# The tail of a two-layer adaptive FFN kernel behind its last convolution: six edits to the order of work

## The chip, the cores and the metric

One core of one Trainium2 chip runs the whole program. The metric is the device time of one execution in microseconds (us); the median of three runs is quoted.

## The reference, cut to what matters

The input x is 128 samples of 32 channels by 512 values. Layer 0 adds to x a gated low-rank product. Layer 1 is what this change touches:

```python
o = conv1d(x1, weight, groups=4, 9 taps) + ctx[:, :, None] + bias      # x1: x after layer 0
xf = o.reshape(-1, 512); N = 4096; capacity = int(3.0 * N / 8)         # 1536
h = relu(layernorm(xf @ gw1.T + gb1) * gamma + beta)
gates = h @ gw2.T + gb2
top_v, top_i = top_k(gates, 2); top_g = softmax(top_v)
onehot = (top_i[..., None] == arange(8)); counts = onehot.sum(axis=0)  # over all 4096 rows
w = einsum('nke,nk,ke->ne', onehot, top_g, counts <= capacity)
out = x1 + xf @ weight.T + einsum(lora_A product * w, lora_B) / 16
```

`counts` runs over every row of the input. So no row's LoRA term can be finished before the routing of the last row is known. The kernel therefore has a loop over all rows and then a separate LoRA stage.

## The kernel before, in words

**Tiling.** A tile is 128 rows (4 samples by 32 channels) by 512 columns, 256 KB. Four tiles (t = 0 to 3) are a step, and there are eight steps (s = 0 to 7). All of y = x1 + main product stays in the on-chip tensor `y_all`, the lora_A products in `tmp_all`, the routing weights in `wst_all`. Each engine has its own instruction list, ordered by hand; semaphores are the only ties between them.

**The loop.** `steps` runs a step function over s. In step 7 and in a closing pass `s == NS` (8) the engines do only what is left: TensorE (PE) finishes convolutions, the gate products `gates(t)`, the transposes of the normed hidden values (`hidden_transposed`), the router product, and the main products. `main(7, t)` is twelve matmuls of 512 columns; their results lie in the banks `ps_last[t]`. `main(7, 2)` is in `ps_t`, `main(7, 1)` and `main(7, 3)` in two `ps_d` banks. A high-and-low split into two fp32r parts (hi is a rounded copy, lo is what is left) gives fp32 quality with three matmuls.

**VectorE (DVE) in step 7.** `norm_first(7)` makes the variance; GpSimd (POOL) takes its root (`rstd`, L483); `y_out(7, 0)` adds a main product into y; `choices_counted(6)` makes the one-hot tensor `oh` (L897) and adds its sums to `cnt` (L904, L905); `norm_last(7)` (L938) scales the hidden values, for which PE waits (L1336); then `choices_weighted(6)`. In the closing pass it makes the choices of step 7.

**ScalarE (ACT) and POOL in step 7.** The last thing that ACT does there is `lb_hi`, a rounded copy of lora_B (L728); POOL's last is the remainder `lb_lo` (L536). `lb_hi` lies in `b_hi`, `lb_lo` in `o1l[0]`.

**Counts.** Behind `main(7, 2)` PE multiplies a matrix of ones with `cnt` (L1464) and four times with a tile of `oh` (L1467), all summed in one bank. In plain fp32 each product is two passes in the trace. `main(7, 3)` follows.

**Behind the loop, DVE:** `allowed` (L1030), the weights of step 0 (L1036, L1037, L1041 which PE transposes), those of step 1 (L1036, L1037, then POOL's product L543), `choices_weighted(7)` (L911 to L915), the weights of steps 2 to 7 (L1036, L1037), then `y_out(7, 1)`, `y_out(7, 2)`, `y_out(7, 3)` (L862) and `lt_lo[0]` (L1051), the remainder of the first transposed weights.

**The LoRA stage.** For each of eight steps PE transposes the weighted products of the next step (L1480) and does three matmuls a tile: `high` (L1487 with `lb_hi`, L1488 with `lb_lo`) and `low` (L1491). In step 0 it does high(0), high(1), low(0), low(1), then waits until all of y is ready and goes on with tiles 2 and 3. ACT makes the transposed hi (L767), POOL the lo (L555). DVE's `finish` adds y to each tile (L1062) and SyncE (SP) stores it (L424).

Of the kernel before, what the change touches and what calls it, by code (L numbers as in the profile page):

```python
# [12 lines left out]
def adaln_ffn_kernel(nc: bass.Bass, x, cond, fside, w0, b0, w1, b1, w2, b2, mixw, mixb, ffa, ffb, ffr,  # L13
# [7 lines left out]
    P = 128  # L21
# [31 lines left out]
    with ctx:  # L53
# [48 lines left out]
        v = sb("v", [P, NT, UC])  # L102
        gms = sb("gms", [P, NT, 2, ER0])
        gm = sb("gm", [P, NT, ER0])
# [74 lines left out]
        def pb(name):  # L179
# [80 lines left out]
        lb_hi, lb_lo = b_hi, o1l[0][:, :, :].rearrange("p q m -> p (q m)")  # L260
        yo = [[xT[:, t, :, :].rearrange("p c m -> p (c m)") for t in range(NT)],
# [64 lines left out]
        def _(sp):  # L326
# [94 lines left out]
            def store(s, par, k):  # L421
                for t in range(NT):
                    sp.wait_ge(s_yo[t], s + 1)
                    sp.dma_start(out_v[bass.ds(s * NT + t, 1)].rearrange("n p h -> p (n h)"), yo[par][t])\  # L424
                      .then_inc(s_out[par][t], 16)
            steps(sp, store, 0, NS - 1)
            for par in range(2):
                for t in range(NT):
                    sp.wait_ge(s_out[par][t], 16 * (NS // 2))

        @block.gpsimd
        def _(pool):
# [77 lines left out]
            def step(s, par, k):  # L510
                if at_step(s, -1):
                    for t in (1, 3):
                        pool.wait_ge(s_x1, t + 1)
                        pool.tensor_copy(xq0[t], y_all[:, t * H:(t + 1) * H].rearrange("p (m q) -> p q m", q=Q))\
                            .then_inc(s_x1q0[t], 1)
                    mixing(1)
                    pool.wait_ge(s_gah, 1)
                    pool.wait_ge(s_gm, 2)
                    pool.tensor_tensor(wt_lo[:, :, H:H + GC], ga[:, :, :], wt_hi[:, :, H:H + GC].bitcast(fp32),
                                       ALU.subtract).then_inc(s_gal, 1)  # L520
                    o1_low(0, 0)
                    return
                if has(s, 2):
                    mixing(s + 2)
                o1_low(s, 1)
                if has(s, -1):
                    rstd(s - 1)
                o1_low(s, 2)
                o1_low(s, 3)
                if has(s, 1):  # L530
                    o1_low(s + 1, 0)
                if at_step(s, NS - 1):
                    rstd(s)
                    pool.wait_ge(s_lbh, 1)
                    pool.wait_ge(s_mp, s * NT + 1)
                    pool.tensor_tensor(lb_lo, lbn, lb_hi[:, :].bitcast(fp32), ALU.subtract).then_inc(s_lb, 1)  # L536
# [23 lines left out]
        def _(act):  # L560
# [81 lines left out]
            def step(s, par, k):  # L642
# [72 lines left out]
                if at_step(s, NS - 1):  # L715
# [58 lines left out]
        def _(dve):  # L774
# [3 lines left out]
            def gates0(u):  # L778
# [27 lines left out]
                wait(dve, s_gtp, u)  # L806
                link(V.tensor_copy(gms[:, :, 0, :].bitcast(fp32r), gm[:, :, :]))
                V.tensor_tensor(gms[:, :, 1, :], gm[:, :, :], gms[:, :, 0, :], ALU.subtract).then_inc(s_gm, 1)
                assert n[0] == N_C0, n[0]
# [83 lines left out]

            def choices_counted(u):
                link, n = chain(dve, s_c2, u * N_C2 + N_C2A)
# [51 lines left out]
            def step(s, par, k):  # L947
# [43 lines left out]
                if at_step(s, NS - 1):  # L991
# [26 lines left out]
                if has(s, -1):  # L1018
# [27 lines left out]
            allow(2, NS).then_inc(s_w, 1)  # L1046
            y_out(NS - 1, 1)
            y_out(NS - 1, 2)
            y_out(NS - 1, 3)
            dve.wait_ge(s_lth, 1)  # L1050
            V.tensor_tensor(lt_lo[0][:, :], ps_a[0][:, :], lt_hi[0][:, :].bitcast(fp32), ALU.subtract)\  # L1051
             .then_inc(s_ltf, 1)


            dve.wait_ge(s_y, NS * NT)

            def finish(s, par, k):
                if has(s, 0):
                    for t in range(NT):
                        dve.wait_ge(s_lp, s * NT + t + 1)  # L1060
                        wait(dve, s_out[par][t], k * 16)
                        V.tensor_tensor(yo[par][t], ps_l[t][:, :], y_all[:, bass.ds(s * ST + t * H, H)],  # L1062
                                        ALU.add).then_inc(s_yo[t], 1)
            steps(dve, finish, 0, NS - 1)

        @block.tensor
        def _(pe):
# [216 lines left out]
            def step(s, par, k):  # L1284
# [31 lines left out]
                def gm_transposed(u):  # L1316
# [6 lines left out]
                    for t in range(NT):  # L1323
                        last = T.transpose(ps_t[:, t * P:(t + 1) * P],
                                           gms[:, t, :, :].rearrange("p a c -> p (a c)"), idp)
                    last.then_inc(s_gtp, 1)
# [147 lines left out]
            def lora(s, par, k):  # L1474
# [8 lines left out]

                def high(t):
                    wait(pe, s_yo[t], s)
                    lhs = lt_hi[par][:, t * P:(t + 1) * P]
                    T.matmul(ps_l[t][:, :], lhs, lb_hi[:, :], start=True, stop=False)  # L1487
                    T.matmul(ps_l[t][:, :], lhs, lb_lo, start=False, stop=False)  # L1488

                def low(t):  # L1490
                    T.matmul(ps_l[t][:, :], lt_lo[par][:, t * P:(t + 1) * P], lb_hi[:, :],  # L1491
                             start=False, stop=True).then_inc(s_lp, 1)
# [17 lines left out]
                if has(s, 0):  # L1510
                    pe.wait_ge(s_ltl, s)
                    for t in range(NT):
                        high(t)
                        low(t)
            steps(pe, lora, -1, NS - 1)

# [25 lines left out]
```

## Time and profile before

| | us |
|---|---|
| median of 3 runs | 305.33 |
| lowest and highest | 303.22, 305.46 |
| the profiled execution | 303.87 |
| its span, first to last instruction | 302.1 |
| PE busy in the span | 290.3 (96%) |
| DVE busy | 194.9 (64%) |
| mean granted TensorE clock | 0.997 |

The busy time of PE counts pipelined matmuls whole, so 96% is how seldom PE stood still, and not how near it was to its peak. 1.73 us of the profiled execution lie around the span.

### The profile page before, as it was taken

How to read it: one execution, taken by the hardware profiler on the slowest of the kernel's cores; microseconds unless marked ns; L12 is line 12 of the kernel's file. 1: busy time of each engine (PE TensorE's matmuls, PEld its weight loads, DVE VectorE, ACT ScalarE, POOL GpSimd, SP SyncE). 2: the span in 40 equal slices, each digit the busy share in tenths (PEclk: the TensorE clock that was granted, in tenths of full speed). 3: DMA queues.
4: the chain of work that ended last, by engine and by line, in shares of the span. 5: the costliest groups of instructions: out<-in, count | busy, mean ns of one | idle time of the engine just before them, and what ended most of it. 6: DMA issues, size and time to landing. Idle time of an engine off the chain costs nothing.

```text
span 302.1 us, 6171 instructions
## 1 busy us (share of the span) xinstructions
PE 290.3 (96%) x1995; PEld 239.7 (79%) x1995; DVE 194.9 (64%) x503; ACT 125.2 (41%) x263; POOL 95.1 (31%) x124
## 2 busy tenths in 40 slices
PE   7999999999999999999999999999999999798994
PEld 6989967787888788879887978797868777586883
DVE  1445984734488448835793579366957645878785
ACT  3417743436523652356235622562256235111330
POOL 4342425132312331143114311431114116216650
PEclk9999999999999999999999999999999999999998
DMA  5696799992779289918892879386538860004887
GB/s 134 196 335 139 169 257 220 235 217 62 218 214 208 54 220 229 192 35 243 207 201 44 242 205 189 55 233 148 136 71 244 174 142 0 0 2 171 322 334 286
DMA packets 74255, 52.75 MB, mean 175 GB/s; under 512 B 44388, under 2 KB 61204, under 8 KB 74232
## 3 DMA queue, kind: packets, MB, share of 16 engines
q1 hardware_dynamic: 72792, 51.37, 67.3%
q10 hardware_dynamic: 1120, 1.07, 1.2%
q0 software_dynamic: 320, 0.02, 0.4%
q8 instruction: 12, 0.20, 0.3%
q14 instruction: 11, 0.09, 0.1%
HBM read 35.67 MB, written 16.78 MB: 174 GB/s over the span
## 4 chain that ended last, share of the span: by engine, by line
PE 65%; SPq 10%; DVE 10%; DMA 6%; issue 4%; ACT 2%; DVEq 0%; ACTq 0%
PE ps_g L1124 13%; PE ps_d L1124 12%; PE ps_c L1264 8%; PE ps_a L1085 6%; PE ps_t L1280 4%; SPq L352 4%; DMA xg<-x1d 3%; PE ps_a L1074 3%; DMA x1d<-xq 3%; PE ps_d L1305 3%; SPq L355 2%; PE ps_d L1306 2%; PE ps_v L1097 2%; PE ps_d L1491 1%; PE ps_d L1487 1%
## 5 line engine op out<-in xcount | busy, mean ns | idle before, releaser
L508 POOL TENSOR_TENSOR o1l<-o,o1h 128x512 fp32r<-128x512 f32 x30 | 39.3, 1311 | 149.3 <-ACT o L639 149.3
L1124 PE MATMUL ps_d<-wt_hi,o1h 128*128 128x336 f32 (+1 forms) x120 | 41.1, 342 | 0.3 <-DVE y_all L950 0.3
L1124 PE MATMUL ps_d<-wt_hi,o1l 128*128 128x336 f32 (+1 forms) x120 | 38.7, 323 | 0.0
L1124 PE MATMUL ps_d<-wt_lo,o1h 128*128 128x336 f32 (+1 forms) x120 | 38.6, 322 | 0.0
L1124 PE MATMUL ps_g<-wt_hi,o1h 128*128 128x336 f32 x112 | 35.7, 319 | 0.6 <-ACT tmp_all L654 0.4
L944 DVE TENSOR_TENSOR oT<-ps_c,biasT 128x512 f32<-128x512 f32 x32 | 21.9, 685 | 21.7 <-PE ps_c L1264 21.7
L1124 PE MATMUL ps_g<-wt_hi,o1l 128*128 128x336 f32 x112 | 35.5, 317 | 0.0
L1124 PE MATMUL ps_g<-wt_lo,o1h 128*128 128x336 f32 x112 | 35.4, 316 | 0.0
L1264 PE MATMUL ps_c<-xg,cw 96*32 96x512 f32 x256 | 34.1, 604 | 1.0 <-DMA xg<-x1d 1.0
L627 ACT ACTIVATE xq<-y_all 128x512 f32 (+1 forms) x29 | 31.8, 1150 | 7.0 <-DMA x1d<-xq 3.7
L1085 PEld LDWEIGHTS ps_a<-pm,xT 128*128 128x128 f32 x256 | 30.2, 192 | 1.4 <-issue 0.8
L1085 PE MATMUL ps_a<-pm,xT 128*128 128x68 f32 x256 | 30.6, 273 | 0.1
L950 DVE TENSOR_TENSOR y_all<-ps_d,xs 128x512 f32 (+1 forms) x24 | 15.9, 689 | 17.9 <-PE ps_d L1306 17.9
L653 ACT ACTIVATE hs<-ps_g 128x32 f32<-128x32 f32 x32 | 6.2, 195 | 49.9 <-DVE y_all L870 49.6
L1280 PEld LDWEIGHTS ps_t<-ident,oT 128*128 128x128 f32 x128 | 14.5, 144 | 15.3 <-issue 14.3
L1124 PEld LDWEIGHTS ps_d<-wt_hi,o1h 128*128 128x128 f32 x120 | 22.7, 189 | 1.0 <-issue 0.7
L1124 PEld LDWEIGHTS ps_d<-wt_lo,o1h 128*128 128x128 f32 x120 | 22.6, 189 | 0.2
L1124 PEld LDWEIGHTS ps_d<-wt_hi,o1l 128*128 128x128 f32 x120 | 22.5, 188 | 0.3
L637 ACT ACTIVATE o1h<-ps_t 128x512 fp32r<-128x512 f32 x30 | 18.0, 599 | 11.1 <-PE ps_t L1280 11.1
L1124 PEld LDWEIGHTS ps_g<-wt_hi,o1h 128*128 128x128 f32 x112 | 21.1, 188 | 1.8 <-issue 1.8
L574 ACT ACTIVATE xT<-ps_a 128x512 f32<-128x512 f32 x32 | 18.2, 604 | 8.1 <-PE ps_a L1074 8.0
L1124 PEld LDWEIGHTS ps_g<-wt_lo,o1h 128*128 128x128 f32 x112 | 21.0, 188 | 0.0
(249 smaller groups left out, 582.1 us busy)
## 6 DMA issues: line engine op xcount, KB each, us to landing
xg<-x1d SPq DMA_DIRECT2D x64, 254.0 KB, 4.8
xg<-x1d SPq DMA_DIRECT2D x32, 256.0 KB, 3.7
x1d<-xq SPq DMA_DIRECT2D x30, 256.0 KB, 3.4
xs<-in_x_dram SPq DMA_DIRECT2D x6, 1024.0 KB, 5.9
out_dram<-xT SPq DMA_DIRECT2D x16, 256.0 KB, 2.1
out_dram<-xg SPq DMA_DIRECT2D x16, 256.0 KB, 2.1
y_all<-in_x_dram ACTq DMA_DIRECT2D x2, 512.0 KB, 5.5
y_all<-in_x_dram SPq DMA_DIRECT2D x1, 1024.0 KB, 5.7
```

The costliest lines, as they stand in the source:

```text
L352: sp.dma_start(taps[i:C:Q, :, 7 - i:7 - i + TAPS], convw.rearrange("o c k -> c o k")).then_inc(s_ld["conv"], 16)
L508: pool.tensor_tensor(lo, o1[t % 2][:, :, :], hi.bitcast(fp32), ALU.subtract).then_inc(s_o1l, 1)
L574: nc.scalar.activation(xT[:, t, :, :].rearrange("p c m -> p (c m)"), ps_a[t % 2][:, :], ACT.Copy).then_inc(s_xt, 1)
L627: nc.scalar.activation(dst, y_all[:, bass.ds(u * ST + t * H, H)].rearrange("p (m q) -> p q m", q=Q), ACT.Copy).then_inc(done, 1)
L637: nc.scalar.activation(o1h[t % 2][:, :, :].rearrange("p q (b o) -> p q b o", o=CG), o_in(t), ACT.Copy).then_inc(s_o1h, 1)
L944: V.tensor_tensor(oT[:, t % 2, :, :], ps_c[:, :].rearrange("p (b m) -> p b m", b=BT), row(biasT[:, bass.ds(u * (NT * BT) + t * BT, BT)], 2 ...
L950: V.tensor_tensor(y_all[:, bass.ds(u * ST + t * H, H)], ps_d[t % 2][:, :], src[:, t, :], ALU.add).then_inc(s_x1, 1)
L1074: last = T.transpose(ps_a[t % 2][:, c * P:(c + 1) * P], bank_x[:, t, c * P:(c + 1) * P], idp)
L1085: last = T.matmul(ps_a[0][:, t * UC:(t + 1) * UC], xT[:, t, c, :], pm[:, c, :], start=(c == 0), stop=(c == HC - 1))
L1124: last = T.matmul(bank[:, 0:columns], a[:, Q - 1 - q, :], w[:, q, first:first + columns], start=(q == 0 and n == 0), stop=(q == Q - 1 and ...
L1264: last = T.matmul(ps_c[C * g:C * g + C, :], cw[0:KC, g, :, :].rearrange("p q o -> p (q o)"), xg[0:KC, t % 2, :, g, :], start=True, stop=True)
L1280: last = T.transpose(ps_t[:, b * P:(b + 1) * P], oT[:, t % 2, b, :], idp)
```

## The change

1. In step 7 `norm_last(7)` runs inside `choices_counted(6)`, ahead of the two instructions that sum `oh` into `cnt`.
2. The four count products on `oh` become one of 64 columns, and `cnt` has columns of its own. DVE now sums the five groups of 16 columns (one new instruction) before the comparison.
3. `y_out(7, 1)` and `y_out(7, 2)` go ahead of the allowed chain on DVE, and `y_out(7, 3)` goes behind `lt_lo[0]`.
4. `lb_hi` and `lb_lo` are made in step 6: ACT's copy ahead of the last `ga_out` of that step, POOL's remainder at the end of its step. `lb_lo` moves to the tensor `gms`, which is declared fp32r for it.
5. The last tile of the LoRA stage is made in two halves of 256 columns, the second in bank `ps_t`: six matmuls in place of three, two additions and two stores in place of one each.

```diff
@@ GpSimd, end of a step
                 if at_step(s, NS - 1):
                     rstd(s)
+                if at_step(s, NS - 2):
                     pool.wait_ge(s_lbh, 1)
-                    pool.wait_ge(s_mp, s * NT + 1)
+                    pool.wait_ge(s_gtp, NS)
                     pool.tensor_tensor(lb_lo, lbn, lb_hi[:, :].bitcast(fp32), ALU.subtract).then_inc(s_lb, 1)
@@ ScalarE, step 7 and the steps before it
                     ga_out(3)
-                    act.wait_ge(s_ld["lora"], 16)
-                    nc.scalar.activation(lb_hi[:, :], lbn, ACT.Copy).then_inc(s_lbh, 1)
                     return
...
                 o_hi(s + 1, 0)
+                if at_step(s, NS - 2):
+                    act.wait_ge(s_ld["lora"], 16)
+                    nc.scalar.activation(lb_hi[:, :], lbn, ACT.Copy).then_inc(s_lbh, 1)
                 ga_out(3)
@@ VectorE
                     link(chosen)
+                    if between is not None:
+                        between()
                     link(V.reduce_sum(cnt1[:, :, :], oh[:, :, :, :].rearrange("p t c e -> p c e t"), AXX))
...
-                    choices_counted(s - 1)
-                    norm_last(s)
+                    choices_counted(s - 1, lambda: norm_last(s))
                     choices_weighted(s - 1)
...
+            y_out(NS - 1, 1)
+            y_out(NS - 1, 2)
             link, n = chain(dve, s_c3, 0)
             dve.wait_ge(s_cntp, 1)
-            link(V.tensor_scalar(allowed[:, :, :], ps_g[:, 0:2 * E1].rearrange("p (c e) -> p c e", c=2),
-                                 float(CAPACITY), None, ALU.is_le))
+            link(V.reduce_sum(cnt1[:, :, :], ps_g[:, 0:2 * E1 * (NT + 1)]
+                              .rearrange("p (t c e) -> p c e t", c=2, e=E1), AXX))
+            link(V.tensor_scalar(allowed[:, :, :], cnt1[:, :, :], float(CAPACITY), None, ALU.is_le))
...
             allow(2, NS).then_inc(s_w, 1)
-            y_out(NS - 1, 1)
-            y_out(NS - 1, 2)
-            y_out(NS - 1, 3)
             dve.wait_ge(s_lth, 1)
             V.tensor_tensor(lt_lo[0][:, :], ps_a[0][:, :], lt_hi[0][:, :].bitcast(fp32), ALU.subtract)\
              .then_inc(s_ltf, 1)
+            y_out(NS - 1, 3)
...
+                        parts = 2 if at_step(s, NS - 1) and t == NT - 1 else 1
+                        n = H // parts
+                        for i in range(parts):
+                            dve.wait_ge(s_lp, s * NT + t + i + 1)
+                            V.tensor_tensor(yo[par][t][:, i * n:i * n + n], (ps_l[t], ps_t)[i][:, i * n:i * n + n],
+                                            y_all[:, bass.ds(s * ST + t * H + i * n, n)],
+                                            ALU.add).then_inc(s_yo[t], 1)
@@ TensorE
-            T.matmul(ps_g[:, 0:2 * E1], ones[:, :], cnt[:, :, :].rearrange("p c e -> p (c e)"), start=True, stop=False)
+            T.matmul(ps_g[:, 2 * E1 * NT:2 * E1 * (NT + 1)], ones[:, :], cnt[:, :, :].rearrange("p c e -> p (c e)"),
+                     start=True, stop=True)
             pe.wait_ge(s_cnt, 1)
-            for t in range(NT):
-                last = T.matmul(ps_g[:, 0:2 * E1], ones[:, :], oh[:, t, :, :].rearrange("p c e -> p (c e)"),
-                                start=False, stop=(t == NT - 1))
-            last.then_inc(s_cntp, 1)
+            T.matmul(ps_g[:, 0:2 * E1 * NT], ones[:, :], oh[:, :, :, :].rearrange("p t c e -> p (t c e)"),
+                     start=True, stop=True).then_inc(s_cntp, 1)
...
+                if at_step(s, NS - 1):
+                    for cols, bank in ((slice(0, H // 2), ps_l[NT - 1]), (slice(H // 2, H), ps_t)):
+                        high(NT - 1, cols, bank)
+                        low(NT - 1, cols, bank)
```

Left out of the diff here: `store` on SP issues the last tile's two halves as two DMAs, and the casts that the new type of `gms` asks for.

## Rows read from the trace of the kernel before

**Rows 1.** Stretches: length, busy PE, PEld, DVE, ACT, POOL, granted clock, DMA share, GB/s

```profile
272.40:273.90 1.50, 0.19 (x2) 0.01 (x1) 1.44 (x3) 0.00 (x0) 1.50 (x3) 1.00 0.00 0
...
274.50:298.30 23.80, 23.73 (x115) 18.93 (x113) 21.01 (x32) 6.52 (x12) 12.18 (x11) 1.00 0.85 317
...
300.00:300.50 0.50, 0.00 (x0) 0.00 (x0) 0.00 (x0) 0.00 (x0) 0.00 (x0) 0.78 1.01 393
```

**Rows 2.** Timeline of step 7: start, length, engine, line, shape [idle before <-releaser]

```profile
256.78 0.63 ACT L728 ACTIVATE b_hi<-xs 128x512 fp32r<-128x512 f32 x1
...
259.00 1.01 POOL L483 TENSOR_TENSOR small<-small,mhalf 128x4 f32<-128x4 f32 x1 [3.76 <-DVE small L931]
...
259.98 1.26 POOL L536 TENSOR_TENSOR o1l<-xs,b_hi 128x512 fp32r<-128x512 f32 x1
...
260.20 1.07 DVE L905 TENSOR_TENSOR cnt<-cnt 128x16 f32<-128x16 f32 x1
...
261.19 0.28 DVE L938 TENSOR_TENSOR hr<-hb,small 128x128 f32<-128x128 f32 x1
...
261.53 0.33 PE L1336 MATMUL ps_a<-ident,hr 128*128 128x128 f32 x1 [1.55 <-DVE hr L938]
...
262.92 0.19 DVE L882 TENSOR_TENSOR sc<-ps_v,gb_b 128x32 f32<-128x32 f32 x1 [0.58 <-PE ps_v L1342]
```

**Rows 3.** All instructions of a line: nanoseconds min/median/max, starts, forms

```profile
L905 DVE TENSOR_TENSOR cnt<-cnt x7: 174/176/1069, 94.7 to 260.2; 128x16 f32<-128x16 f32 x7
...
L904 DVE TENSOR_REDUCE cnt<-oh x7: 257/258/261, 94.4 to 259.9; 128x16 f32<-128x64 f32 x7
```

**Rows 4.** Timeline of PE from the counts to the first transposes

```profile
265.97 0.39 PE L1124 MATMUL ps_t<-wt_hi,wt_lo 128*128 128x512 f32 x1
...
266.31 0.97 PEld L1467 LDWEIGHTS ps_g<-oh,ones 128*128 128x128 f32 x8
...
267.20 0.19 PEld L1124 LDWEIGHTS ps_d<-wt_hi,gmT 128*128 128x128 f32 x1
...
269.87 1.03 PEld L1480 LDWEIGHTS ps_a<-ident,xs 128*128 128x128 f32 x8
```

**Rows 5.** Timeline of DVE and POOL behind the counts

```profile
267.49 0.17 DVE L1030 TENSOR_SCALAR allowed<-ps_g 128x16 f32<-128x16 f32 x1 [1.84 <-PE ps_g L1467]
...
268.19 0.69 DVE L1041 TENSOR_TENSOR xs<-tmp_all,wst_all 128x512 f32<-128x512 f32 x1
...
269.32 1.06 POOL L543 TENSOR_TENSOR xs<-tmp_all,wst_all 128x512 f32<-128x512 f32 x1 [8.08 <-DVE wst_all L1037]
...
271.08 0.36 DVE L1037 TENSOR_TENSOR wst_all<-wst_all 128x192 f32<-128x192 f32 x1
...
271.36 0.68 DVE L862 TENSOR_TENSOR y_all<-ps_d,y_all 128x512 f32<-128x512 f32 x1
...
273.16 0.68 DVE L1051 TENSOR_TENSOR wt_lo<-ps_a,wt_hi 128x512 fp32r<-128x512 f32 x1
```

**Rows 6.** Timeline of PE, first tiles of the LoRA stage

```profile
271.39 0.50 PE L1487 MATMUL ps_c<-b_hi,wt_hi 128*128 128x512 f32 x1 [0.25 <-ACT wt_hi L767]
...
271.72 0.39 PE L1488 MATMUL ps_c<-o1l,wt_hi 128*128 128x512 f32 x1
...
273.89 0.50 PE L1491 MATMUL ps_c<-b_hi,wt_lo 128*128 128x512 f32 x1 [1.31 <-DVE wt_lo L1051]
...
274.69 0.40 PE L1488 MATMUL ps_d<-o1l,wt_hi 128*128 128x512 f32 x1
```

**Rows 7.** Timeline of step 6's end: ACT and POOL

```profile
247.16 0.20 ACT L653 ACTIVATE hs<-ps_g 128x32 f32<-128x32 f32 x1 [2.98 <-DVE y_all L870]
...
249.53 1.28 POOL L508 TENSOR_TENSOR o1l<-o,o1h 128x512 fp32r<-128x512 f32 x1 [3.98 <-ACT o L639]
```

**Rows 8.** The load of lora_B by its source line

```profile
L408 SPq DMA_DIRECT2D xs<-in_L_ffn_lora_B_dram x1: 340/340/340, 205.1 to 205.1; - x1
```

**Rows 9.** Timeline of DVE: an addition of 336 columns out of PSUM

```profile
244.95 0.51 DVE L867 TENSOR_TENSOR y_all<-ps_d,y_all 128x336 f32<-128x336 f32 x1 [1.72 <-PE ps_d L1124]
```

More of the change, by code:

```diff
@@ L102, in adaln_ffn_kernel @@
         v = sb("v", [P, NT, UC])
-        gms = sb("gms", [P, NT, 2, ER0])
+        gms = sb("gms", [P, NT, 2, ER0], fp32r)
         gm = sb("gm", [P, NT, ER0])
@@ L259, in adaln_ffn_kernel @@
                                       for i in range(2)]
-        lb_hi, lb_lo = b_hi, o1l[0][:, :, :].rearrange("p q m -> p (q m)")
+        lb_hi, lb_lo = b_hi, gms[:, :, :, :].rearrange("p t a c -> p (t a c)")
         yo = [[xT[:, t, :, :].rearrange("p c m -> p (c m)") for t in range(NT)],
@@ L422, in store @@
                 for t in range(NT):
-                    sp.wait_ge(s_yo[t], s + 1)
-                    sp.dma_start(out_v[bass.ds(s * NT + t, 1)].rearrange("n p h -> p (n h)"), yo[par][t])\
-                      .then_inc(s_out[par][t], 16)
+                    parts = 2 if at_step(s, NS - 1) and t == NT - 1 else 1
+                    n = H // parts
+                    for i in range(parts):
+                        sp.wait_ge(s_yo[t], s + i + 1)
+                        sp.dma_start(out_v[bass.ds(s * NT + t, 1)].rearrange("n p h -> p (n h)")[:, i * n:i * n + n],
+                                     yo[par][t][:, i * n:i * n + n]).then_inc(s_out[par][t], 16)
             steps(sp, store, 0, NS - 1)
@@ L428, in _ @@
                 for t in range(NT):
-                    sp.wait_ge(s_out[par][t], 16 * (NS // 2))
+                    sp.wait_ge(s_out[par][t], 16 * (NS // 2 + (par == 1 and t == NT - 1)))
         @block.gpsimd
@@ L806, in gates0 @@
                 wait(dve, s_gtp, u)
-                link(V.tensor_copy(gms[:, :, 0, :].bitcast(fp32r), gm[:, :, :]))
-                V.tensor_tensor(gms[:, :, 1, :], gm[:, :, :], gms[:, :, 0, :], ALU.subtract).then_inc(s_gm, 1)
+                link(V.tensor_copy(gms[:, :, 0, :], gm[:, :, :]))
+                V.tensor_tensor(gms[:, :, 1, :], gm[:, :, :], gms[:, :, 0, :].bitcast(fp32),
+                                ALU.subtract).then_inc(s_gm, 1)
                 assert n[0] == N_C0, n[0]
@@ L892, in choices_first, with choices_counted @@
                 assert n[0] == N_C2A, n[0]
-            def choices_counted(u):
+            def choices_counted(u, between=None):
                 link, n = chain(dve, s_c2, u * N_C2 + N_C2A)
@@ L1059, in finish @@
                     for t in range(NT):
-                        dve.wait_ge(s_lp, s * NT + t + 1)
                         wait(dve, s_out[par][t], k * 16)
-                        V.tensor_tensor(yo[par][t], ps_l[t][:, :], y_all[:, bass.ds(s * ST + t * H, H)],
-                                        ALU.add).then_inc(s_yo[t], 1)
+                        parts = 2 if at_step(s, NS - 1) and t == NT - 1 else 1
+                        n = H // parts
+                        for i in range(parts):
+                            dve.wait_ge(s_lp, s * NT + t + i + 1)
+                            V.tensor_tensor(yo[par][t][:, i * n:i * n + n], (ps_l[t], ps_t)[i][:, i * n:i * n + n],
+                                            y_all[:, bass.ds(s * ST + t * H + i * n, n)],
+                                            ALU.add).then_inc(s_yo[t], 1)
             steps(dve, finish, 0, NS - 1)
@@ L1324, in gm_transposed @@
                         last = T.transpose(ps_t[:, t * P:(t + 1) * P],
-                                           gms[:, t, :, :].rearrange("p a c -> p (a c)"), idp)
+                                           gms[:, t, :, :].bitcast(fp32).rearrange("p a c -> p (a c)"), idp)
                     last.then_inc(s_gtp, 1)
@@ L1482, in weighted_transposed, with high, low @@
                     last.then_inc(s_ltp, 1)
-                def high(t):
+                def high(t, cols=slice(0, H), bank=None):
                     wait(pe, s_yo[t], s)
                     lhs = lt_hi[par][:, t * P:(t + 1) * P]
[L1487 to L1491, printed above, removed]
+                    bank = bank or ps_l[t]
+                    T.matmul(bank[:, cols], lhs, lb_hi[:, cols], start=True, stop=False)
+                    T.matmul(bank[:, cols], lhs, lb_lo[:, cols], start=False, stop=False)
+                def low(t, cols=slice(0, H), bank=None):
+                    bank = bank or ps_l[t]
+                    T.matmul(bank[:, cols], lt_lo[par][:, t * P:(t + 1) * P], lb_hi[:, cols],
                              start=False, stop=True).then_inc(s_lp, 1)
@@ L1511, in lora @@
                     pe.wait_ge(s_ltl, s)
-                    for t in range(NT):
+                    for t in range(NT - 1 if at_step(s, NS - 1) else NT):
                         high(t)
                         low(t)
+                if at_step(s, NS - 1):
+                    for cols, bank in ((slice(0, H // 2), ps_l[NT - 1]), (slice(H // 2, H), ps_t)):
+                        high(NT - 1, cols, bank)
+                        low(NT - 1, cols, bank)
             steps(pe, lora, -1, NS - 1)
```

## The prediction, made before the changed kernel was run

> **What bounds the kernel now.** I read the granted clock first: it is full until the last matmul, so the clock explains nothing. Then the timeline of the tail, where brackets give an engine's idle time and who ended it, and the busy time by stretch. From step 7 on TensorE (PE) is the bound, with two real holes. The first is 1.55 us ahead of the transposes of the normed values (L1336), released by DVE's L938 [rows 2]. The second is 1.31 us ahead of low(0) (L1491), released by DVE's `lt_lo` L1051 [rows 6]; in that stretch PE is busy 0.19 of 1.50 us [rows 1]. A third cost is no hole but small work: ten weight loads for the counts between `main(7, 2)` and `main(7, 3)`. Behind 274.5 PE is busy 23.73 of 23.80 us [rows 1]: the LoRA stage takes its PE time, whenever it begins. So the change is worth what it lets PE begin that stage earlier, plus or minus the last store.
>
> Why the first hole is as long as it is can be read from four rows. POOL's root ends at 260.01, and `norm_last` needs only that. But ahead of it on DVE stands L905, 16 elements, which takes 1.07 us from 260.20, while the line's median is 0.176 us [rows 2, 3]. POOL's `lb_lo` (L536) runs from 259.98 to 261.24, and L905 ends when it ends [rows 2]. L904, which starts in the same stretch, has its usual length in all seven executions [rows 3]. The Trainium skill, page "SBUF — State Buffer", section "Who interferes with whom", says that a DVE instruction with two SBUF inputs and a GpSimd one that reads SBUF block each other for a whole instruction, and that a reduction never does. The trace agrees for both lines.
>
> **Edits 1 and 4, norm ahead of the counts and the split earlier.** Each alone would remove most of the hole: with L536 gone L905 is short, and with L938 ahead of it its length doesn't delay PE. Together L938 starts as soon as the root is there: 260.01 + 0.03 = 260.04 in place of 261.19, 1.15 us earlier, and the transposes start at 260.38. PE has nothing to do from 259.98, so the gain is on its path: **1.15 us**. About 0.4 us of the hole stay. Behind L938 now stand L904 and L905, 0.26 and 0.18 long [rows 3], ahead of the weights of step 6. With L938 at 260.04 the weights begin at about 260.75. Before they began right behind L938, at 261.4. So they gain some 0.65 us where PE gains 1.15, and the other 0.5 comes out of the 0.58 us that DVE was idle ahead of the last choices [rows 2]. That idle time just suffices.
>
> The moved work: ACT's copy of 0.63 us and POOL's of 1.26 us [rows 2]. In step 6 ACT is idle for 2.98 us up to 247.16 and POOL for 3.98 us up to 249.53 [rows 7]. The copy fits at 244.2 to 244.8. POOL's previous instruction ends at 249.53 - 3.98 = 245.55, so `lb_lo` fits until 246.8, 2.7 us ahead of POOL's next work. The load of lora_B was issued at 205.1 [rows 8], some 39 us ahead, so ACT's new wait holds up nothing: behind it stand `ga_out(3)` and the next `o_hi`, and PE waits for those. DVE's additions there read one tensor in PSUM. Cost: **0**; without this cover up to 0.63 + 1.26 = 1.89 us. The semaphore waits that allow the new places (step 7's gate transposes done) are passed on PE early in step 6, so they cost nothing.
>
> **Edit 2, counts.** Ten passes become four. Eight weight loads take 267.20 - 266.31 = 0.89 us [rows 4], 0.11 each, so six fewer give **0.67 us** on PE. The pass of 64 columns isn't in the trace: at least 0.11 (16 columns), at most the 23.80 / 115 = 0.21 us of a mostly 512-column stretch [rows 1]; two passes then cost up to 0.2 more. I take 0.11, since 64 is nearer to 16. PE's first transposes behind `main(7, 3)` move from 269.87 [rows 4] by 1.15 + 0.67 = 1.82 us to 268.05.
>
> DVE pays for it with a reduction of 80 elements out of PSUM. The nearest rows are the reduction L904 of 64 elements, 0.26 us [rows 3], below it a comparison of 16 out of PSUM, 0.17, and above it an addition of 192 elements, 0.36 [rows 5]. L904 is nearest: I take 0.28, and 0.03 to the next instruction, **0.31 us**, with 0.17 and 0.4 as bounds.
>
> **Edit 3, the additions.** Before, DVE is idle for 1.84 us until 267.49 for the counts [rows 5]. `y_out(7, 1)` fits in there whole. `y_out(7, 2)` needs `main(7, 2)`, whose last matmul ends at 265.97 + 0.39 = 266.36 [rows 4], less 1.15 = 265.21, and starts at 265.26. Three additions take 273.16 - 271.36 = 1.80 us [rows 5], so 0.60 each, and the reduction starts at 265.86. The counts are in PSUM at about 265.6, so this addition costs the chain some 0.2 to 0.3 us. Then `allowed` starts at 265.86 + 0.31 = 266.17, **1.32 us** earlier than 267.49. L1041 ends at 268.88 - 1.32 = 267.56 and PE wants it at 268.05, so it still doesn't wait. POOL's L543 moves with the chain, from 269.32 to 268.00, and ends at 269.06; PE's second transposes wait for it and end at 269.6, when high(0) begins (before: 271.39 [rows 6]).
>
> From here on DVE is late, and it decides. Its last L1037 starts at 271.08 - 1.32 = 269.76, and what follows it at 271.36 - 1.32 = 270.04 [rows 5]. Before, that was three additions and then L1051 at 273.16. Now it is L1051 itself: 270.04, **3.12 us** earlier. PE's low(0) goes from 273.89 to 270.77, while its high products are done at 270.4: 0.4 us of the hole of 1.31 stay. `y_out(7, 3)` starts 0.60 later, at 270.64, and ends at 271.32. PE waits for all of y ahead of high(2) and is done with low(1) at 271.1, so a new wait of 0.2 to 0.3 us opens. High(2) starts at 271.39; a first matmul behind a wait delays the next by 0.33 (271.39 to 271.72 [rows 6]), so its second is at 271.73 in place of 274.69 [rows 6]: **2.96 us**. The sum on PE is 1.82, and the rest, 1.14, comes from the second hole, of which small pieces of wait remain.
>
> **Edit 5, halves.** PE and DVE: an addition of 512 columns takes 0.68 and one of 336 columns 0.51 [rows 5, 9], so 256 take about 0.43. DVE's second half ends about when the whole tile did, 298.97 in the old time. The second store has half the bytes, worth up to 0.35 us. But the DMA engines are fully busy from 300.0 to 300.5, at 393 GB/s [rows 1], more than a microsecond after DVE is done: the last step's stores wait for bandwidth and not for DVE. At that rate 256 KB take 0.67 us, as long as DVE takes to make them. The bytes are the same, so I take **0**, bounds -0.35 and +0.2 (double the packets, at half the size). The Trainium skill, page "SBUF — State Buffer", section "Summary: rules for kernel authors", gives about 358 GB/s for transfers to HBM. By that figure a tile would take, as an estimate, 0.73 us, and halves would give nothing either; the trace shows somewhat more than the page.
>
> **The sum.** 2.96 + 0 = 2.96 us off the profiled 303.87, which is 300.91. The profiled execution lies 1.46 under the median; the saving is taken off the median: 305.33 - 2.96 = **302.4**.
>
> **The rivals.**
> (a) DVE's chain is longer than I have it. It decides from `main(7, 2)` on, with no slack, so each 0.1 us there is 0.1 at the end: a reduction of 0.4, and L905 slow for a reason of its own. Then `oh` of step 7 comes 0.9 - 0.1 = 0.8 later and with it the first addition, at 265.3 in place of 264.5, so the reduction starts at 266.6 in place of 265.86. For it: L905 alone carries the proof of POOL's hold. Against it: its median in six other steps [rows 3]. L905 slow would give 2.96 - 0.75 = 2.2 us saved, 303.1; both of it 2.1, 303.2.
> (b) The stores gain. The halves shorten the last landing by 0.35, and a DMA engine that ran behind the others doesn't: 3.3 to 3.6 saved, 301.7 to 302.0. Against it: the full DMA share [rows 1].
> (c) The change doesn't do its work in the LoRA stage: if the stores bounded it, an earlier begin would give nothing but the wait to the end. Against it: a DMA share of 0.85 beside 23.73 of 23.80 on PE [rows 1]. 0 saved, 305.3.
> (d) Slower than before: the moved split is in the way in step 6. POOL takes its list in order, so `lb_lo` waiting for ACT holds back `o1_low(7, 1)`, `main(7, ...)` and all behind. It decides if `lb_hi` comes later than 244.8 + 2.7 = 247.5, and loses more than is gained from 250.5 on, which a late load of lora_B or ACT stuck behind its wait could do; at 252 it costs 4.5 - 2.96 = 1.5 us, 306.9. Against it: 39 us between issue and use [rows 8], and the idle times [rows 7].
>
> **How the numbers follow.** Forecast 0.64, (a) 0.17, (b) 0.12, (c) 0.03, (d) 0.04. For the range: (b) at the low end and (a) at the high end, and the median of before lies anywhere between 303.22 and 305.46, which moves the end results by a microsecond downward: 300.3 to 304.3. One per cent is 3.05 us, about what a measurement of this kernel can tell from no change, and the forecast of 2.96 lies just under it. Of its 0.64 the scatter of some 0.3 us puts 0.28 above and 0.36 below; with (b) above, and (a), (c) and the milder part of (d) within: faster by over 1% 0.40, within 1% 0.57, slower 0.03.
>
> **What would show it.** L938 starts within 0.1 us of the end of POOL's root, L905 takes 0.18 us, PE idles about 0.4 us ahead of L1336. Four weight loads stand between the main products of tiles 2 and 3. `allowed` is preceded by one reduction of about 0.3 us and no idle time of DVE. low(0) is 3.1 us earlier and high(2) has a short wait for DVE's y. The last store's landing moves with PE's last matmul. I am wrong if any DVE instruction behind the counts is stretched, if ACT or POOL wait in step 6, or if the last landing doesn't follow PE.

## The result, and the profile after

The changed kernel takes 301.05 us (median of 7, 300.46 to 302.11), the kernel before 305.01 us (median of 7, 303.22 to 308.09). The ratio is 0.9895 with a 95% interval of 0.9863 to 0.9927: 1.05% faster. The profiled execution took 301.39 us with a span of 299.7; before it was 303.87 and 302.1. Disturbed executions, more than 1.5% above the fastest of the same kernel, are left out of all ratios, among them the 308.09 us of the kernel before; without it the median of that kernel is 304.28 us.

Absolute times of two executions differ by some tenths before the change begins, so I count from the start of POOL's root of step 7: 259.00 before [rows 2], 259.22 after. **D** is the time from there to the second matmul of high(2): 274.69 - 259.00 = 15.69 us before [rows 6].

The timeline of the changed kernel, around the last norm; L946 is the old L938, L913 the old L905, L1348 the old L1336:

```profile
259.22 1.01 POOL L486 TENSOR_TENSOR small<-small,mhalf 128x4 f32<-128x4 f32 x1 [3.75 <-DVE small L939]
...
260.32 0.29 DVE L946 TENSOR_TENSOR hr<-hb,small 128x128 f32<-128x128 f32 x1 [0.22 <-POOL small L486]
...
260.66 0.33 PE L1348 MATMUL ps_a<-ident,hr 128*128 128x128 f32 x1 [0.47 <-DVE hr L946]
...
260.81 0.17 DVE L913 TENSOR_TENSOR cnt<-cnt 128x16 f32<-128x16 f32 x1
```

DVE's L946 starts 1.10 us behind the root's start, where L938 started 2.19 behind it [rows 2]. L913 takes 0.17 us and not 1.07. PE idles 0.47 us and not 1.55.

The same timeline behind the counts. L1039 is the new reduction, L1041 `allowed`, L547 POOL's weights of step 1, L923 the last step of `choices_weighted(7)`, L1058 `lt_lo`, L868 `y_out`, L1504, L1499 and L1500 low, high with `lb_hi` and high with `lb_lo`:

```profile
265.55 0.69 DVE L868 TENSOR_TENSOR y_all<-ps_t,y_all 128x512 f32<-128x512 f32 x1
...
266.16 0.23 DVE L1039 TENSOR_REDUCE cnt<-ps_g 128x16 f32<-128x80 f32 x1
...
266.43 0.17 DVE L1041 TENSOR_SCALAR allowed<-cnt 128x16 f32<-128x16 f32 x1
...
268.26 1.06 POOL L547 TENSOR_TENSOR xs<-tmp_all,wst_all 128x512 f32<-128x512 f32 x1 [8.03 <-DVE wst_all L1047]
...
268.82 0.58 DVE L923 SCALAR_TENSOR_TENSOR wst_all<-exs,small 128x64 f32<-128x64 f32 x1
...
269.37 0.66 PE L1491 MATMUL ps_a<-ident,xs 128*128 128x128 f32 x4 [0.19 <-POOL xs L547]
...
270.30 0.68 DVE L1058 TENSOR_TENSOR wt_lo<-ps_a,wt_hi 128x512 fp32r<-128x512 f32 x1
...
270.90 0.68 DVE L868 TENSOR_TENSOR y_all<-ps_d,y_all 128x512 f32<-128x512 f32 x1
...
271.04 0.50 PE L1504 MATMUL ps_c<-b_hi,wt_lo 128*128 128x512 f32 x1
...
271.64 0.50 PE L1499 MATMUL ps_d<-b_hi,wt_hi 128*128 128x512 f32 x1
...
271.98 0.40 PE L1500 MATMUL ps_d<-gms,wt_hi 128*128 128x512 f32 x1
```

Nothing on DVE waits between 265.55 and 270.90: it is the bound there. One piece of it is the hold of step 7 once more. L923 has 64 elements and two SBUF inputs; it takes 0.58 us beside POOL's L547, which ends at 269.32, and 0.23 us as the median of its eight executions. The kernel before has the same 0.58. So some 0.35 us of DVE's deciding chain may still be had; no run tried it. `lt_lo` starts 11.08 us behind the root in place of 14.16 [rows 5]. D is 271.98 - 259.22 = 12.76 us, **2.93 us less** than before; the forecast was 2.96.

The busy time by stretch (columns as in [rows 1]):

```profile
271.64:295.60 23.96, 23.86 (x118) 19.38 (x117) 21.17 (x32) 6.52 (x12) 14.01 (x12) 1.00 0.85 315
...
297.50:298.00 0.50, 0.00 (x0) 0.00 (x0) 0.00 (x0) 0.00 (x0) 0.00 (x0) 1.00 0.93 309
...
298.00:298.50 0.50, 0.00 (x0) 0.00 (x0) 0.00 (x0) 0.00 (x0) 0.00 (x0) 1.00 0.07 12
```

The LoRA stage is as before, PE busy 23.86 of 23.96 us, DMA share 0.85. Its last PE instruction ends 36.28 us behind the root (before 39.24), again 2.96 less. The span ends 2.70 us earlier (40.44 behind the root, before 43.14), so 0.26 us are lost behind PE, and the row from 298.0 on shows a thin tail of transfers (the last two figures of a row are the DMA share and GB/s).

### The profile page after: what moved, and what is told of

Same layout as the page of the kernel before. It is cut to its first block, busy times and chain, and to the rows that moved or that the text cites. A ratio compares the mean times of both kernels' runs of the same rounds, so it can differ in the third digit from the quotient of the medians.

```text
span 299.7 us, 6154 instructions
## 1 busy us (share of the span) xinstructions
PE 289.8 (97%) x1992; PEld 239.0 (80%) x1992; DVE 194.4 (65%) x505; ACT 125.3 (42%) x263; POOL 95.2 (32%) x124
## 3 DMA queue, kind: packets, MB, share of 16 engines
q10 hardware_dynamic: 1120, 1.07, 1.2%
## 4 chain that ended last, share of the span: by engine, by line
PE 66%; SPq 10%; DVE 8%; DMA 6%; issue 4%; ACT 2%; POOL 1%; DVEq 0%; ACTq 0%
PE ps_g L1136 13%; PE ps_d L1136 12%; PE ps_c L1276 8%; PE ps_a L1097 7%; PE ps_t L1292 4%; DMA xg<-x1d 3%; SPq L352 3%; PE ps_a L1086 3%; DMA x1d<-xq 3%; PE ps_d L1317 3%; SPq L355 2%; PE ps_d L1318 2%; PE ps_v L1109 2%; PE ps_d L1499 1%; PE ps_d L1504 1%
```

## The experiments

Each was run beside the kernel before on the same chip. D and the other distances are counted from the start of the root of step 7 in its own trace.

### The split of lora_B alone

```diff
@@ kernel before: edit 4 only
-                    pool.wait_ge(s_mp, s * NT + 1)
+                if at_step(s, NS - 2):
+                    pool.wait_ge(s_gtp, NS)
```

> The kernel before with edit 4 alone (lora_B split in step 6). Measure D: from the start of POOL's root of step 7 to the second matmul of high(2) in the LoRA stage; before 274.69 - 259.00 = 15.69 us. Theory (POOL's subtraction holds back L905): L905 takes 0.18 us, L938 starts 0.8 us earlier, D = 14.9, time 0.8 us under before. Rival (L905 is slow there for a reason of its own): L905 still takes about 1 us, D = 15.7, time as before. Rival (the moved split is in the way in step 6): ACT or POOL end their step-6 work later and the root comes later.

Measured: ratio 0.994 [0.9914, 0.9967], which is 1.8 us where 0.8 was expected; most of the excess goes with the clock (under "The median against the profile"), for among the executions with a mean clock above 0.995 the medians are 302.88 and 303.66 us, 0.8 apart. Timeline, L908 being the old L905 and L941 the old L938:

```profile
258.34 1.01 POOL L483 TENSOR_TENSOR small<-small,mhalf 128x4 f32<-128x4 f32 x1 [3.76 <-DVE small L934]
...
259.54 0.18 DVE L908 TENSOR_TENSOR cnt<-cnt 128x16 f32<-128x16 f32 x1
...
259.63 0.28 DVE L941 TENSOR_TENSOR hr<-hb,small 128x128 f32<-128x128 f32 x1
...
259.98 0.33 PE L1339 MATMUL ps_a<-ident,hr 128*128 128x128 f32 x1 [0.66 <-DVE hr L941]
```

L908 takes 0.18 us, so the length of L905 was POOL's doing. L941 starts 1.29 us behind the root (before 2.19), and the transposes 1.64 behind it (before 2.53): 0.89 us earlier. D is 15.28, but in this trace PE ran at half clock for 3.4 us within the stretch (shown below for another run), so D is of no use here. The root comes no later than before (258.34, before 259.00): ACT and POOL had room in step 6.

### The norm ahead of the counts alone

```diff
@@ kernel before: edit 1 only
-                    choices_counted(s - 1)
-                    norm_last(s)
+                    choices_counted(s - 1, lambda: norm_last(s))
```

> The kernel before with edit 1 alone (L938 ahead of L904 and L905; POOL's lb_lo still in step 7). Theory: L938 starts 0.03 us behind the root, PE's transposes 1.15 us earlier; L905 starts near 260.5 and is stretched to POOL's end, so it takes about 0.75 us and not 1.07; the last choices are late by some 0.4 us against PE, and PE has just enough other work; D = 14.6, time 1.1 us under before. Rival (L905 slow for a reason of its own): L905 takes its 1.07 us whole, the one-hot tensor is another 0.3 late and PE waits at the counts, D = 14.9.

Measured: 0.9992 [0.9951, 1.0033], D = 15.63. Neither expectation holds. Timeline, L940 being the old L938:

```profile
259.17 1.01 POOL L483 TENSOR_TENSOR small<-small,mhalf 128x4 f32<-128x4 f32 x1 [3.76 <-DVE small L933]
...
260.15 1.26 POOL L536 TENSOR_TENSOR o1l<-xs,b_hi 128x512 fp32r<-128x512 f32 x1
...
260.27 1.29 DVE L940 TENSOR_TENSOR hr<-hb,small 128x128 f32<-128x128 f32 x1 [0.23 <-POOL small L483]
...
261.61 0.33 PE L1337 MATMUL ps_a<-ident,hr 128*128 128x128 f32 x1 [1.47 <-DVE hr L940]
```

POOL starts its subtraction (L536) at 260.15, DVE its norm at 260.27. L940, which reads two tensors in SBUF, takes 1.29 us in place of 0.28 and ends 0.15 us behind POOL. The blocked instruction is not L905 as such; it is whichever DVE instruction of that kind comes next behind POOL's start. The edit moves the block from L905 to the norm itself, and PE gains 0.09 us.

### The counts alone

```diff
@@ kernel before: edit 2 only
-            for t in range(NT):
-                last = T.matmul(ps_g[:, 0:2 * E1], ones[:, :], oh[:, t, ...])
+            T.matmul(ps_g[:, 0:2 * E1 * NT], ones[:, :], oh[:, :, :, :].rearrange("p t c e -> p (t c e)"), ...)
```

> The kernel before with edit 2 alone (one count product, a reduction on DVE). Theory (behind the counts DVE decides): PE saves 0.67 us, the comparison L1030 starts only 0.3 us earlier since the reduction stands ahead of it, D = 15.4, time 0.3 us under before. Rival (PE's work decides): D = 15.0.

Measured: 0.9986 [0.9956, 1.0016], which agrees with 0.3 us and can't exclude 0.7. D is 16.91, longer than before, and the busy time by stretch of this kernel says why (the granted clock is the third figure from the end):

```profile
259.90:261.40 1.50, 0.00 (x0) 0.00 (x0) 1.47 (x4) 0.00 (x0) 1.26 (x2) 1.00 0.00 0
...
261.50:262.80 1.30, 1.30 (x7) 0.97 (x8) 0.65 (x4) 0.46 (x1) 0.00 (x0) 1.00 0.00 0
...
262.80:266.20 3.40, 3.40 (x9) 2.63 (x9) 2.53 (x9) 0.23 (x1) 0.00 (x0) 0.50 0.00 0
...
266.20:268.00 1.80, 1.80 (x11) 1.50 (x10) 0.00 (x0) 0.00 (x0) 0.00 (x0) 0.99 0.04 9
```

1.4 us behind the first hole the granted clock fell to 0.50, that is 1.2 GHz, for 3.4 us. In that time matmuls of 512 columns start 0.43 us apart, and 0.23 us apart ahead of it and behind it. D can't be read here. The next experiment answers this edit better.

### The changed kernel without the counts' edit

```diff
@@ changed kernel: edit 2 undone
-            link(V.reduce_sum(cnt1[:, :, :], ps_g[:, 0:2 * E1 * (NT + 1)] ...
```

> The changed kernel with edit 2 undone (ten passes for the counts on PE, no reduction on DVE). Theory: PE loses 0.67 us at the counts; DVE waits for them with both additions done, and the comparison starts 0.2 us later than in the changed kernel, 7.4 us behind the root in place of 7.21; D = 13.0 in place of 12.76, so the edit is worth 0.2 to 0.3 us of its 0.67. Rival: D = 13.4.

Measured: 0.992 [0.9881, 0.9959]; D = 13.05, as the theory has it (rival 13.4). The comparison and high(0) start here, the root being at 258.35:

```profile
265.69 0.17 DVE L1039 TENSOR_SCALAR allowed<-ps_g 128x16 f32<-128x16 f32 x1 [0.33 <-PE ps_g L1478]
...
269.66 0.50 PE L1499 MATMUL ps_c<-b_hi,wt_hi 128*128 128x512 f32 x1 [0.25 <-ACT wt_hi L772]
```

The comparison is 7.34 us behind the root, against 7.21 in the changed kernel. High(0) is 11.31 behind it, against 10.65: there the 0.67 us that PE saves are whole. But in the changed kernel the weight loads of low(0) and high(2) then wait 0.41 and 0.30 us for DVE, and in this run for nothing. So the edit is worth 0.3 us of the 0.67, since with it DVE decides, its reduction being part of that chain.

### The additions alone

```diff
@@ kernel before: edit 3 only
+            y_out(NS - 1, 1)
+            y_out(NS - 1, 2)
             link, n = chain(dve, s_c3, 0)
...
             .then_inc(s_ltf, 1)
+            y_out(NS - 1, 3)
```

> The kernel before with edit 3 alone (two additions of y ahead of the comparison, the third behind lt_lo). Theory: both additions fit into DVE's idle 1.84 us, the comparison keeps its place, low(0) follows high(1) without a hole, a short wait of about 0.1 to 0.3 us opens ahead of high(2); D = 14.1, time 1.6 us under before. Rival (the additions delay the comparison by their length): D = 14.7 or more.

Measured: 0.9949 [0.9919, 0.9978]: 1.6 us. In this trace the granted clock was 0.50 from 40.4 to 50.6 us, which is why all of it is later, and 1.00 in the stretch read here. Timeline: the root, the comparison, `lt_lo`, the addition, low(0) and the second matmul of high(2):

```profile
264.69 1.01 POOL L483 TENSOR_TENSOR small<-small,mhalf 128x4 f32<-128x4 f32 x1 [3.77 <-DVE small L931]
...
273.13 0.17 DVE L1032 TENSOR_SCALAR allowed<-ps_g 128x16 f32<-128x16 f32 x1 [0.33 <-PE ps_g L1467]
...
277.09 0.69 DVE L1050 TENSOR_TENSOR wt_lo<-ps_a,wt_hi 128x512 fp32r<-128x512 f32 x1
...
277.70 0.68 DVE L862 TENSOR_TENSOR y_all<-ps_d,y_all 128x512 f32<-128x512 f32 x1
...
278.14 0.40 PE L1491 MATMUL ps_c<-b_hi,wt_lo 128*128 128x512 f32 x1
...
278.85 0.39 PE L1488 MATMUL ps_d<-o1l,wt_hi 128*128 128x512 f32 x1
```

The comparison starts 8.44 us behind the root (8.49 before): both additions fit into DVE's idle time. low(0) has no wait. D = 14.16, 1.53 less than before.

### The changed kernel without the additions' edit

```diff
@@ changed kernel: edit 3 undone
-            y_out(NS - 1, 1)
-            y_out(NS - 1, 2)
             link, n = chain(dve, s_c3, 0)
```

> The changed kernel with edit 3 undone. Theory: DVE's chain decides the end. The comparison starts 0.2 to 0.3 us earlier than in the changed kernel, for y_out(7, 2) no longer stands ahead of the reduction, but three additions stand ahead of lt_lo again; D = 14.2 (changed kernel 271.98 - 259.22 = 12.76), time 1.4 us over the changed kernel. Rival (the PE work saved is worth its 1.82 us by itself): D = 13.9 or less.

Measured: 0.9963 [0.9934, 0.9991], D = 14.27, as expected; the changed kernel's 0.9895 is 2.1 us lower, where 1.4 were expected (among executions with a mean clock above 0.995 the medians are 302.97 and, in the later run of the changed kernel, 301.34, 1.6 apart). The granted clock was 0.50 from 40.2 to 50.5 us and 1.00 in the stretch read here. Timeline: the root, the comparison, `lt_lo` and low(0):

```profile
264.11 1.01 POOL L486 TENSOR_TENSOR small<-small,mhalf 128x4 f32<-128x4 f32 x1 [3.75 <-DVE small L939]
...
271.16 0.17 DVE L1039 TENSOR_SCALAR allowed<-cnt 128x16 f32<-128x16 f32 x1
...
276.83 0.68 DVE L1059 TENSOR_TENSOR wt_lo<-ps_a,wt_hi 128x512 fp32r<-128x512 f32 x1
...
277.57 0.50 PE L1504 MATMUL ps_c<-b_hi,wt_lo 128*128 128x512 f32 x1 [1.62 <-DVE wt_lo L1059]
```

The comparison starts 7.05 us behind the root (7.21 in the changed kernel), `lt_lo` 12.72 (11.08), and the hole ahead of low(0) is 1.62 us, longer than before any change. PE alone had saved 1.8 us; 1.42 of D come out.

### The last tile whole, twice

```diff
@@ changed kernel: edit 5 undone
-                    parts = 2 if at_step(s, NS - 1) and t == NT - 1 else 1
+                    parts = 1
```

> The changed kernel with edit 5 undone (last tile whole). Theory (the last step's stores wait for DMA bandwidth): the last landing keeps its distance to PE within 0.1 us, and the time is that of the changed kernel within 0.2 us. Rival (halves shorten the end): 0.35 us longer. Rival (halves cost, by double the packets and a second issue): 0.2 us shorter.

Measured: 300.2 us, ratio 0.9861 [0.9833, 0.9888], where the changed kernel has 0.9895. To settle it both were run again side by side:

> The changed kernel as it is, beside its variants on one chip. It and whole_again answer whether the halves cost something: whole_last_tile measured 0.9861 [0.9833, 0.9888] of before, the changed kernel 0.9895 [0.9863, 0.9927]. Theory (bandwidth): the two agree within 0.2 us, and what differed was one DMA engine that ended 0.67 us behind the others in one profile and not in the other. Rival (halves cost): this kernel is 0.5 to 0.9 us slower than whole_again.

> The changed kernel with edit 5 undone, once more, beside after_again. Theory: its time within 0.2 us. Rival (halves cost): 0.5 to 0.9 us under after_again, and all 16 DMA engines end together again where the changed kernel has one that ends 0.67 us behind.

Measured: halves 301.34 us, 0.9895 [0.9856, 0.9933]; whole 300.37 us, 0.9862 [0.9826, 0.9899]. In 13 executions with halves the fastest took 300.41 us, in 12 with the tile whole the slowest took 300.93, and the medians differ by 0.85 and 0.97. The theory of no effect falls: the kernel with halves is 0.9 us slower. PE is not it: D is 12.74 and 12.75, and PE's last instruction ends 36.32 and 36.31 us behind the root. The busy time by stretch shows the difference, first with halves (root at 259.21):

```profile
297.60:297.90 0.30, 0.00 (x0) 0.00 (x0) 0.00 (x0) 0.00 (x0) 0.00 (x0) 1.00 1.04 348
...
298.20:298.50 0.30, 0.00 (x0) 0.00 (x0) 0.00 (x0) 0.00 (x0) 0.00 (x0) 0.63 0.09 14
...
298.50:298.80 0.30, 0.00 (x0) 0.00 (x0) 0.00 (x0) 0.00 (x0) 0.00 (x0) 0.50 0.04 10
```

then with the tile whole (root at 258.95):

```profile
297.60:297.90 0.30, 0.00 (x0) 0.00 (x0) 0.00 (x0) 0.00 (x0) 0.00 (x0) 1.00 0.17 55
...
297.90:298.20 0.30, 0.00 (x0) 0.00 (x0) 0.00 (x0) 0.00 (x0) 0.00 (x0) 0.71 0.00 0
```

With halves the transfers thin out instead of ending: a share of 0.04 to 0.09 is about one of 16 engines at work, until 298.73. Fifteen engines have ended 38.89 us behind the root, the last one ends at 39.53. With the tile whole the sixteen end between 38.66 and 38.82, the last one 0.03 us behind the fifteenth. So of the 0.71 us between the last landings 0.64 are one DMA engine that is behind, and 0.1 is the rest. The trace doesn't name the engine of a packet, but it names the queue. The changed kernel from 290 to 299:

```profile
q1 hardware_dynamic: 1707, 2.84, 86.0%
...
q14 instruction: 1, 0.01, 0.3%
```

and with the tile whole until its last landing:

```profile
q1 hardware_dynamic: 1526, 2.77, 90.8%
```

In the changed kernel one packet of 8 KB on the instruction queue falls among the last stores (at 297.7, taking 0.4 us). With the tile whole it comes at 299.7, beyond the span. The kernel before has it among its stores too (297.97, last engine 0.62 behind the others). Of the 13 traces in which all stores go through SP, ten have the packet ahead of the last landing, and in each of them one engine ends 0.35 to 0.87 us behind the other fifteen (seven of them between 0.52 and 0.67). In the three that have it behind the last landing (whole twice, and the run without the counts' edit, which does have halves) the last engine is 0.02 to 0.03 us behind the fifteenth. In that run with halves the last landing comes 2.56 us behind PE's end, with the tile whole 2.51 (`whole_again`), and in the changed kernel 3.21 (`after_again`): halves by themselves cost about 0.05 us.

That the packet is the cause is inferred from this agreement; no run moved it by itself, and three things don't fit well. The packet takes 0.31 to 0.42 us, so its own length doesn't explain a lag of up to 0.87. In the run named `better` below a second engine is 0.29 us behind the other fourteen, with no packet of its own on that queue. And the one execution with halves and no late engine took no less time for it: 301.16 us with a span of 298.3, so 2.8 us lie around the span, where it is 1.7 in the changed kernel.

### The second half from another queue

```diff
@@ changed kernel: the last half is stored by ScalarE
+            act.wait_ge(s_yo[NT - 1], NS + 1)
+            act.dma_start(out_v[NS * NT - 1][:, H // 2:H], yo[1][NT - 1][:, H // 2:H])
```

> The changed kernel, the second half of the last tile stored from ScalarE's DMA queue instead of SP's. In the changed kernel that half is ready at 296.24 and SP issues it at 296.5, behind its previous issue. Theory (bandwidth): the last landing doesn't move by more than 0.1 us. Rival (SP's issue decides): it comes 0.25 us earlier.

SP leaves this half out. Measured: median 301.6 us (301.17 of the six that the ratio counts), 0.9911 [0.9877, 0.9944], no gain. In its trace (granted clock 0.50 from 41.3 to 51.5 us, 1.00 in the tail until the last landing) the last landing comes 39.30 us behind the root in place of 39.51, so the theory's 0.1 us falls by the letter and the rival's 0.25 comes near. But fifteen engines have ended at 38.86, against 38.84: what is shorter is the lag of the last one, 0.44 in place of 0.67, and the span ends at 40.81 in place of 40.44. SP's issue isn't what the fifteen wait for; whether it is part of the last one's lag isn't shown.

### One more order for DVE, with halves and whole

```diff
@@ changed kernel
-            allow(1, 2).then_inc(s_w, 1)
+            allow(1, 3).then_inc(s_w, 1)
             choices_weighted(NS - 1)
-            allow(2, NS).then_inc(s_w, 1)
...
             y_out(NS - 1, 3)
+            allow(3, NS).then_inc(s_w, 1)
```

> The changed kernel with DVE's order behind the counts changed once more: the weights of step 2 are made with those of step 1, and those of steps 3 to 7 only behind lt_lo and y_out(7, 3). Theory (the two pieces of wait that are left ahead of low(0) and high(2) are DVE's): both go, D = 12.3 in place of 12.76, time 0.4 us under the changed kernel. Rival: the wait moves to POOL's product of step 3 or to DVE's first additions of the LoRA stage, D = 12.3 but the last matmul gains less.

> The order of the run named better (step 2's weights early, the rest behind lt_lo and the last addition) with the last tile whole. Theory: the last matmul starts where better's did or earlier (36.20 us behind the root, against 35.90 in whole_last_tile), since the gain of 0.37 us at high(2) was lost again to POOL's remainder of step 1, stretched from 1.28 to 1.45 us and begun late: the time is that of whole_again within 0.3 us. Rival: 0.3 us faster than whole_again.

Measured: with halves 301.22 us, 0.9898 [0.9868, 0.9928]; whole 301.96 us, 0.9905 [0.987, 0.9939]. D is 12.39 and 12.38, as expected, but the rival's second half came too: the last matmul starts 36.20 and 36.08 us behind the root, later than the 36.00 and 35.91 of their counterparts. The whole version is 1.6 us slower than `whole_again`, far more than PE's 0.17, so the theory of 0.3 us falls. Its last engine ends 0.49 us behind the others and the span another 1.51 behind that (0.82 in `whole_again`); what makes the span end so late isn't shown. Where PE's gain goes is in the timeline of the version with halves:

```profile
270.94 1.45 POOL L559 TENSOR_TENSOR wt_lo<-xs,wt_hi 128x512 fp32r<-128x512 f32 x1 [0.90 <-ACT xs L774]
...
271.27 1.30 DVE L1047 TENSOR_TENSOR wst_all<-wst_all 128x160 f32<-128x160 f32 x1
...
272.49 0.68 DVE L1073 TENSOR_TENSOR xT<-ps_c,y_all 128x512 f32<-128x512 f32 x1
...
273.32 0.47 PE L1499 MATMUL ps_c<-b_hi,wt_hi 128*128 128x512 f32 x1 [0.32 <-DVE xT L1073]
```

The last weights (L1047, two SBUF inputs) start at 271.27 while POOL's L559 has run since 270.94, and take 1.30 us; by the 0.19 us of 32 elements and the 0.36 of 192, I estimate some 0.3 for 160. So DVE's first addition of the LoRA stage starts at 272.49, and PE waits for it at 273.32. The moved instruction ran into the same block that edit 4 had removed elsewhere.

## Why the prediction came out right, and where its steps failed

The time moved by 1.05% where 0.97% was forecast (2.96 of 303.87), and 301.05 lies in the range of 300.3 to 304.3. The mechanism on PE came as described, 2.93 us of 2.96. The closeness of the whole is in part luck. The forecast of 302.4 is 1.35 above the measured median; 1.05 of that is its base, a median of three runs at 305.33 where six give 304.28. And two things that I had not foreseen pull opposite ways: the end of the stores takes from the gain, and the clock adds to it (both below).

**Edits 1 and 4.** L938 came 1.09 us earlier behind the root where I had 1.15, the hole kept 0.47 where I had 0.4, and L905 fell to 0.17. The sentence "Each alone would remove most of the hole" is wrong in one half. The split alone gives 0.89 us of it; the norm alone gives 0.09, since the norm's own instruction (L938, L940 in that run) is then held for 1.29 us. I had seen POOL hold L905 and not asked who stands there once the order changes. The rule that I had quoted from the Trainium skill, page "SBUF — State Buffer", section "Who interferes with whom", is about two SBUF inputs, and L938 has two like L905. So the gain at the first hole is edit 4's, and edit 1 adds 0.2 to it, once L905 is short. Rival (a)'s "L905 slow for a reason of its own" falls.

**Edit 4's cover.** ACT ran the copy at 244.29 to 244.92 and POOL the remainder at 245.74 to 247.03, 2.7 us ahead of its next work at 249.75. Cost 0, as forecast; rival (d) falls.

**Edit 2.** The pass of 64 columns cost little more than one of 16, as forecast: the four passes start at 265.36 and `main(7, 3)` at 265.72, 0.36 us for them where the ten took 1.03, so all of the 0.67 was saved. The reduction took 0.23 us (0.28 forecast). The comparison came 1.28 us earlier behind the root, with 1.32 forecast.

**Edit 3.** `lt_lo` came 3.08 us earlier (3.12), and a wait for y opened ahead of high(2), as described. By the runs above the edits give about 0.9 (4), 0.2 (1), 0.3 (2) and 1.5 us (3), together 2.9 of the 2.93.

**Edit 5 is the term that was mis-sized.** I took 0 with bounds of -0.35 and +0.2, from the full DMA share. That part held: without the engine that is behind, halves cost 0.1 us or less. Against the same kernel with the tile whole they cost 0.9. Against the kernel before the cost is small, because that one has its last DMA engine 0.62 us behind too; that is why the forecast of the whole change still came out, which is luck. I had seen the full DMA share and taken it for all of the end. The thin tail of the kernel before would have told me that the end belonged to one engine:

```profile
300.50:301.00 0.50, 0.00 (x0) 0.00 (x0) 0.00 (x0) 0.00 (x0) 0.00 (x0) 0.50 0.14 49
...
301.00:301.50 0.50, 0.00 (x0) 0.00 (x0) 0.00 (x0) 0.00 (x0) 0.00 (x0) 0.50 0.03 12
```

Rival (b) named that engine and gave its going a gain. With halves it stayed behind. With the tile whole it was not, and the span ends 39.64 us behind the root: 3.50 us less than before, within (b)'s 3.3 to 3.6, though (b) expected it of the halves.

**The median against the profile.** The profiled executions differ by 2.48 us (2.70 with the roots aligned) and the medians by 3.96, or 3.23 without the 308.09. Over three groups of runs of the kernel before, 21 of the 62 executions that the ratios count have a mean granted clock of 0.995 or less and a median of 305.62 us, and the other 41 have 303.65. Of 13 executions of the changed kernel none has it, nor has any of the 12 with the tile whole. Two of the traces that the ratios count have such a mean, and both show 3.4 us at half clock: behind the first hole in the run of the counts alone, and at 272.6, behind the second (1.3 us), in that of the split alone. I had read the full clock of one trace and written that it "explains nothing". It explains nothing of that execution, and about 2 us in one of three others, which is 0.7 us on a mean. Among executions with a mean above 0.995 alone, the second run of the changed kernel has a median of 301.34 us and the kernel before, beside it, 303.76: 2.42 us, or 0.8%, is what the order of work gave, and about 0.7 us more goes with the clock. Whether the shorter holes prevent it isn't shown: the run without the counts' edit has small holes and 2 of its 8 executions show the low mean.

## What to carry to other kernels

When an instruction of one engine holds back one of another, as POOL's subtraction did here, the hold can fall on whichever instruction of that kind comes next. Before reordering the one that is held, ask what will stand in its place, and rather move the holder. A saving on the busiest engine is worth only what the next one lets through: here DVE let through 0.3 of the 0.67 us at the counts and gave 1.5 us for moving additions into idle time. For a last tile, look at when each DMA engine ends, not at the mean share, before splitting it.

## What the runs showed of the hardware that I had not expected

- A DVE instruction of 128 elements with two SBUF inputs took 1.29 us in place of 0.28 when it started 0.12 us behind a POOL subtraction of 1.26 us; one of 160 elements took 1.30. The reduction L904, which overlapped the same POOL instruction before, kept its 0.26.
- One 8 KB packet on the instruction queue among saturated stores went with one of 16 DMA engines ending 0.35 to 0.87 us behind the others (eleven of eleven traces), and its absence with a last engine 0.02 to 0.03 us behind the fifteenth (three of three). With the tile whole, or without the counts' edit, it came behind the stores.
- The granted clock fell to 1.2 GHz for 3.4 us, 0.2 and 1.4 us behind a hole of 1.3 and 1.5 us on PE, in two traces; the trace of the kernel before has both holes and the full clock. Executions with the low mean took 2 us more.
- A whole store of 256 KB takes 2.0 to 2.1 us from issue to landing, also when the 16 engines are saturated and none is behind.
